# Gather and scatter interleaved tile by tile on TensorE, and all target one-hots loaded instead of three of eight made by VectorE

## What is computed

```python
# block 0: five layers over the edges
h = leaky(x @ W1[l] + b1[l]) @ W2[l] + b2[l]
e = leaky(edge_attr @ We1[l] + be1[l]) @ We2[l] + be2[l]
msg = h[src] * e * dot_scale[l]
agg = segment_sum(msg, dst, num_segments=n)
x = layernorm(x + agg * res_w[l]) * ln_g[l] + ln_b[l]
...
# block 3: one more pass over the edges
msgs = relu(node_inputs[src] + edge_inputs)
agg = segment_sum(msgs, dst, num_segments=n)
```

## Time and profile before

| what | value |
|---|---|
| median of 3 runs | 7844.31 us (7841.6 to 7846.52) |
| the profiled execution | 7817.12 us, its span 7815.2 us |
| PE matmul busy | 6285.5 us (80%) |
| PE weight load busy | 5013.5 us (64%) |
| VectorE busy | 5308.1 us (68%) |
| ScalarE busy | 2933.7 us (38%) |
| GpSimd busy | 2771.1 us (35%) |
| HBM | read 815.28 MB, written 278.78 MB |

### The profile page before, as it was taken

One profiled execution on the slowest core, in us unless ns is written; L12 is line 12 of the kernel. 1 busy time (PEld: TensorE's weight loads), 2 busy tenths in 40 slices (PEclk: granted clock), 3 DMA queues, 4 the chain that ended last, 5 costly groups with the idle time before them and its releaser, 6 DMA issues. The chain is left out here.

```text
span 7815.2 us, 276543 instructions
## 1 busy us (share of the span) xinstructions
PE 6285.5 (80%) x87510; PEld 5013.5 (64%) x87511; DVE 5308.1 (68%) x15345; ACT 2933.7 (38%) x5054; POOL 2771.1 (35%) x4280
## 2 busy tenths in 40 slices
PE   4888888846666588788788788788789998999887
PEld 3666666634444377677677677677776776777676
DVE  7555554579999777677677677677865554555677
ACT  2444444424444433333333333233653332333333
POOL 2666666643333144344344344344000000000343
PEclk9888888865555699899899899799768998999999
DMA  2666666622222577577577577577441111111576
GB/s 78 172 180 181 182 179 177 182 72 73 71 73 71 187 191 191 140 193 196 138 196 193 139 193 196 133 194 192 158 178 51 68 60 44 68 60 60 138 202 174
DMA packets 1403296, 1098.82 MB, mean 141 GB/s; under 512 B 1012406, under 2 KB 1171821, under 8 KB 1393467
## 3 DMA queue, kind: packets, MB, share of 16 engines
q1 hardware_dynamic: 887994, 797.65, 33.3%
q0 software_dynamic: 224768, 240.90, 12.7%
q10 hardware_dynamic: 290304, 57.05, 4.0%
HBM read 815.28 MB, written 278.78 MB: 140 GB/s over the span
## 5 line engine op out<-in xcount | busy, mean ns | idle before, releaser
L544 POOL DMA_DIRECT2D big<-rows x2592 | 1415.2, 546 | 3721.9 <-issue 2284.6
L1309 PE MATMUL ps<-big 128*128 128x64 bf16 x20736 | 1292.7, 198 | 377.7 <-issue 356.3
L1296 PE MATMUL ps<-big 128*128 128x64 bf16 x41472 | 1418.2, 196 | 100.2 <-DVE big L1783 57.5
L1296 PEld LDWEIGHTS ps<-big 128*128 128x128 fp8e4 x41472 | 1338.4, 100 | 175.4 <-issue 135.5
L1309 PEld LDWEIGHTS ps<-big 128*128 128x128 bf16 x20736 | 985.7, 99 | 643.9 <-issue 431.1
L814 POOL DMA_INDIRECT rows<-big x800 | 1022.9, 1279 | 606.3 <-issue 360.9
L1018 ACT CAST big<-big 128x512 bf16<-128x512 f32 x720 | 445.1, 618 | 1293.4 <-DVE big L1796 1230.4
L1796 DVE TENSOR_TENSOR big<-ps,big 128x512 f32<-128x512 f32 x720 | 497.8, 691 | 608.3 <-PE ps L1296 594.1
L1255 PE MATMUL ps<-identb,big 128*128 128x128 bf16 x2304 | 472.6, 308 | 359.9 <-DVE big L1684 353.6
L1573 DVE SCALAR_TENSOR_TENSOR big<-big 128x1000 f32<-128x1000 f32 (+1 forms) x300 | 359.5, 1198 | 579.1 <-ACT big L905 435.5
L1212 PEld LDWEIGHTS ps<-big 128*125 128x125 f32 (+1 forms) x4800 | 682.6, 212 | 101.5 <-issue 57.6
(11 more groups left out here) (263 smaller groups left out, 9350.4 us busy)
## 6 DMA issues: line engine op xcount, KB each, us to landing
big<-ohsD SPq DMA_DIRECT2D x432, 512.0 KB, 3.7
big<-ohdD SPq DMA_DIRECT2D x432, 320.0 KB, 4.1
big<-rows POOLq DMA_DIRECT2D x2592, 32.0 KB, 3.6
big<-rows SPq DMA_DIRECT2D x2592, 32.0 KB, 3.5
big<-maskD SPq DMA_DIRECT2D x50, 1600.0 KB, 6.7
big<-rows ACTq DMA_DIRECT2D x1728, 32.0 KB, 3.3
big<-keyT SPq DMA_DIRECT2D x100, 488.3 KB
maskD<-big SPq DMA_DIRECT2D x25, 1600.0 KB, 6.2
```

Source lines behind the costliest of these rows:

```text
L544: eng.dma_start(edge[:, s.r, j, :], rows[bass.ds(v[s.r * (hi - lo) + j - lo], P), col]).then_inc(landed[s.r], 16)
L1296: last = pe.matmul(pG[g.r][:, j * D:(j + 1) * D], ohsR[:, g.r, at:at + P].bitcast(F8), slices[:, g.r, q // QUAD, (3 * k + c) * D:(3 * k + ...
L1309: last = pe.matmul(pacc[:, bass.ds(w[j], D)], hot[:, g.r, j * P:(j + 1) * P], parts[:, g.r, c, j * D:(j + 1) * D], start=False, stop=False ...
```

## The change

The target one-hots of all eight tiles are stored in `ohdD` and loaded in each pass; `remake`, its semaphore `hot_made`, and POOL's `dstl` go. An `ohdD` load of two groups grows from 320 to 512 KB, and so does its share of the stores in the unpacking stage. On TensorE, `turn_over` takes the place of `scatter` and `gather`: both sets of waits stand at the start of a step, and then for each tile j come the six gather matmuls of group s - 1 and the three scatter matmuls of group s - 5. `gathered` is signalled by the last gather matmul, which is three matmuls before the step's end. The lags, buffers and all other engines' loops are as before.

```diff
@@ -74,8 +74,6 @@
 CW = NP // CUTS
 NQ = TILES // QUAD
 RAW = 3
-KEEP = 5
-MADE = GT - KEEP
 TURNS = -(-W // 4)
 CTS = 4
 ROWSUMS = 11
@@ -113,7 +111,7 @@
         keyT = dram("keyT", (ET, EP))
         blkT = dram("blkT", (ET, EP), BF16)
         ohsD = dram("ohsD", (NG, P, 2 * GT * P), U8)
-        ohdD = dram("ohdD", (NG, P, KEEP * P), BF16)
+        ohdD = dram("ohdD", (NG, P, GT * P), BF16)
         maskD = dram("maskD", (W, P, NP))
         cntD = dram("cntD", (W, P, NP), U16)
...
@@ -405,7 +398,6 @@
         res_ready = sem("res_ready")
         mid_ready = sem("mid_ready")
         lo_ready = sem("lo_ready")
-        hot_made = sem("hot_made")
         hot_loaded = [sem(f"hot_loaded{r}") for r in range(RING // 2)]
         craw_loaded = [sem(f"craw_loaded{r}") for r in range(RAW)]
         over_made = sem("over_made")
@@ -660,7 +652,7 @@
                 sp.wait_ge(hots_ready, i * 2 + 2)
                 hold(sp)
                 sp.dma_start(ohdD[bass.ds(i, 1)].rearrange("o p f -> (o p) f"),
-                             ohD[:, r % 2, 0:KEEP, :].rearrange("p a b -> p (a b)")).then_inc(dst_stored[r % 2], 16)
+                             ohD[:, r % 2, :, :].rearrange("p a b -> p (a b)")).then_inc(dst_stored[r % 2], 16)
 
...
@@ -697,7 +689,7 @@
                 if not s.known or s.i >= RING:
                     sp.wait_ge(scattered, base + s.lag(RING).i + 2)
                     hold(sp)
-                sp.dma_start(hot[:, s.r:s.r + 2, 0:KEEP * P], ohdD[bass.ds(s.i, 2)].rearrange("g p f -> p g f")).then_inc(hot_loaded[s.r // 2], 16)
+                sp.dma_start(hot[:, s.r:s.r + 2, :], ohdD[bass.ds(s.i, 2)].rearrange("g p f -> p g f")).then_inc(hot_loaded[s.r // 2], 16)
 
             def load_pass(base, col):
...
@@ -828,7 +820,6 @@
                     pool.wait_ge(hots_ready, i * 2 - 2)
                     hold(pool)
                 span = bass.ds(i * GT, GT)
-                pool.tensor_tensor(dstl[:, span], rowst[:, r, :, 1], valid[:, span], ALU.mult)
                 for k in range(2):
                     last = pool.tensor_tensor(idm[:, r % 2, k * GT:(k + 1) * GT], rowst[:, r, :, k], valid[:, span], ALU.mult)
                 last.then_inc(ids_masked, 1)
@@ -1280,35 +1271,49 @@
                 for b in range(4):
                     pe.matmul(bank(b), zerob[:, :], zerob[:, 0:1].to_broadcast([P, 512]), start=True, stop=False, skip_group_check=True)
 
-            def gather(s, base, nth):
+            def gather_ready(g, base, nth):
+                pe.wait_ge(ohs_loaded[g.r // 2], (nth * TRIPS + g.t) * 16 + 16)
+                pe.wait_ge(sliced, base + g.i + 1)
+                if not g.known or g.i >= RING:
+                    pe.wait_ge(m_ready, base + g.lag(RING).i + 1)
+                hold(pe)
+
+            def gather(g, j):
+                q = j // QUAD
+                for k in range(2):
+                    at = ((q * 2 + k) * QUAD + j % QUAD) * P
+                    for c in range(3):
+                        last = pe.matmul(pG[g.r][:, j * D:(j + 1) * D], ohsR[:, g.r, at:at + P].bitcast(F8),
+                                         slices[:, g.r, q, (3 * k + c) * D:(3 * k + c + 1) * D],
+                                         start=(k + c == 0), stop=(k + c == 3))
+                return last
+
+            def scatter_ready(g, base, nth):
+                pe.wait_ge(lo_ready, base + g.i + 1)
+                pe.wait_ge(hot_loaded[g.r // 2], (nth * TRIPS + g.t) * 16 + 16)
+
+            def scatter(g, j, w):
+                for c in range(3):
+                    last = pe.matmul(pacc[:, bass.ds(w[j], D)], hot[:, g.r, j * P:(j + 1) * P], parts[:, g.r, c, j * D:(j + 1) * D],
+                                     start=False, stop=False, skip_group_check=True)
+                return last
+
+            def turn_over(s, w, base, nth):
+
+                to, of = s.lag(S_LAG), s.lag(G_LAG)
+                if s.live(S_LAG):
+                    scatter_ready(to, base, nth)
                 if s.live(G_LAG):
-                    g = s.lag(G_LAG)
-                    pe.wait_ge(ohs_loaded[g.r // 2], (nth * TRIPS + g.t) * 16 + 16)
-                    pe.wait_ge(sliced, base + g.i + 1)
-                    if not g.known or g.i >= RING:
-                        pe.wait_ge(m_ready, base + g.lag(RING).i + 1)
-                    hold(pe)
-                    for q in range(0, GT, QUAD):
-                        for j in range(q, q + QUAD):
-                            for k in range(2):
-                                at = ((q // QUAD * 2 + k) * QUAD + j - q) * P
-                                for c in range(3):
-                                    last = pe.matmul(pG[g.r][:, j * D:(j + 1) * D], ohsR[:, g.r, at:at + P].bitcast(F8),
-                                                     slices[:, g.r, q // QUAD, (3 * k + c) * D:(3 * k + c + 1) * D],
-                                                     start=(k + c == 0), stop=(k + c == 3))
-                    last.then_inc(gathered, 1)
-
-            def scatter(s, w, base, nth):
+                    gather_ready(of, base, nth)
+                for j in range(GT):
+                    if s.live(G_LAG):
+                        got = gather(of, j)
+                    if s.live(S_LAG):
+                        put = scatter(to, j, w)
+                if s.live(G_LAG):
+                    got.then_inc(gathered, 1)
                 if s.live(S_LAG):
-                    g = s.lag(S_LAG)
-                    pe.wait_ge(lo_ready, base + g.i + 1)
-                    pe.wait_ge(hot_made, base + g.i + 1)
-                    pe.wait_ge(hot_loaded[g.r // 2], (nth * TRIPS + g.t) * 16 + 16)
-                    for j in range(GT):
-                        for c in range(3):
-                            last = pe.matmul(pacc[:, bass.ds(w[j], D)], hot[:, g.r, j * P:(j + 1) * P], parts[:, g.r, c, j * D:(j + 1) * D],
-                                             start=False, stop=False, skip_group_check=True)
-                    last.then_inc(scattered, 1)
+                    put.then_inc(scattered, 1)
 
             with pe.Fori(0, LAYERS) as l:
                 pe.wait_ge(x_ready, l + 1)
@@ -1341,8 +1346,7 @@
                 def body(s):
                     if s.r % 2 == 0:
                         two[:] = blocks(PE, s.i)
-                    scatter(s, two[s.r % 2], l * NG, l)
-                    gather(s, l * NG, l)
+                    turn_over(s, two[s.r % 2], l * NG, l)
 
                 steps(pe, body)
                 pe.drain().then_inc(summed, 1)
...
@@ -1759,15 +1762,6 @@
                 dve.tensor_tensor(tabp[2], tres, tabp[1], ALU.subtract).then_inc(tab_lo, 1)
                 dve.wait_ge(tab_lo, nth + 1)
 
-            def remake(s, base):
-                if s.live(2):
-                    g = s.lag(2)
-                    if not g.known or g.i >= RING:
-                        dve.wait_ge(scattered, base + g.lag(RING).i + 1)
-                        hold(dve)
-                    dve.tensor_tensor(hot[:, g.r, KEEP * P:].rearrange("p (a b) -> p a b", a=MADE), each(iota1b[:, 0:P], MADE),
-                                      over(dstl[:, bass.ds(g.i * GT + KEEP, MADE)], P), ALU.is_equal).then_inc(hot_made, 1)
@@ -1843,7 +1837,6 @@
                     message(s, l * NG, "edge", l)
                     rest(s, l * NG, "edge")
                     lower(s, l * NG)
-                    remake(s, l * NG)
 
                 steps(dve, body)
                 lc = Chain(dve, l_chain, l * END)
```

More of the change, by code:

```diff
@@ L255, in graph_kernel @@
         ohsT = carve(2, 2 * GT * P, dt=U8)
-        dstl = big[:, BIG - TILES // 2:].bitcast(BF16)
         dq = carve(NQ, 2)
@@ L261, in graph_kernel @@
         total = carve(W)
-        assert carve.at[0] <= BIG - TILES // 2
         rowjunk = ps[:, 0:NP]
@@ L1356, in body @@
                         two[:] = blocks(PE, s.i)
-                    scatter(s, two[s.r % 2], base, nth)
-                    gather(s, base, nth)
+                    turn_over(s, two[s.r % 2], base, nth)
                 steps(pe, body)
@@ L1867, in body @@
                     lower(s, base)
-                    remake(s, base)
                 steps(dve, body)
```

## The result

The changed kernel takes 7546.07 us (median of 4 runs, 7504.43 to 7555.36) against 7845.42 us for the kernel before (4 runs, 7841.6 to 7849.61): a ratio of 0.9608, 95% interval 0.9571 to 0.9645. The forecast was 7475 us in a range of 7380 to 7680, so the sign and the range held, and 71 of the 370 us didn't come.

The account below looks back on a forecast made before the run. PE's own instruction stream was taken as the bound; with four limits near 12, layers at 12.4 us a turn (305 less) and the last pass at 11.7 (65 less) give 370 us less: 7475 us, range 7380 to 7680.

Parts of the forecast that it names:

- PE's instruction stream as the bound: Edge passes: scatter's register instructions starve the array, about 180 ns a tile for 88 ns of matmuls; interleaving hides them.
- Rival (b): Scatter's register instructions aren't hidden by the interleaving, PE keeps 14.1 us a turn: 7844 us, within 15; chance 0.07.
- PE's floor of 12.0 a turn: Layers: interleaving lowers PE's floor from 14.1 to about 12.0 us a turn, bounds 11.4 and 14.1; last pass near 11.6.
- VectorE's relief: Edge passes: one-hots no longer made give nothing alone; VectorE's floor falls from about 2.7 to 2.2 us a group.
- SyncE's 12.05 us a turn: Layers: SyncE's own issuing work doesn't shrink, so no turn can be shorter than 12.05 us; last pass 10.7.
- The late load: Edge passes: larger ohdD loads land 4.8 to 5.3 us after issue instead of 4.1; turn of 11.9 to 12.7 us.
- rival (a): DMA engines or late ohdD loads hold the loop at about 13.2 us a turn: 7664 us; chance 0.18.
- Rival (c): Slower: ohdD landing lengthens the loop from 7.0 us on; with 8 us, 8060 us in all; chance 0.06.
- DMA traffic: Edge passes: engine work grows from 41.2 to 45.9 engine-us a group, a floor of 11.5 us a turn.
- Unpacking: Unpacking stage: POOL loses a small operation and ohdD stores grow; zero, at most 5 us either way.
- The sum: Layers 305 us less and last pass 65 less, together 370 less: 7475 us; chance 0.69.
- 12.4 a turn: Layers: four limits near 12 (12.0, 12.05, 11.5, 11.9 to 12.7) don't overlap perfectly, so 12.4 us a turn was taken.

Follow-up runs that it names:

- Fixed addresses: Kernel before, old order, but scatter tile j adds into block j, without PE's register instructions and table reads (target block choice left out): 7348.99 us, 0.9396.
- four loaded: Kernel before with the interleaved TensorE order, four target one-hots of eight loaded and four made by VectorE: 7388.22 us, 0.9438 against the kernel before.
- five: Kernel before with the interleaved TensorE order alone, five target one-hots loaded and three made by VectorE as before: 7420.49 us, 0.9491.
- edges ahead: Changed kernel with ScalarE's two edge loads issued one group earlier, some from wrong rows: 7494.33 us, 0.9597 against the kernel before.

## Why the prediction was right, and where it was off

**PE's instruction stream as the bound: right.** Fixed addresses bring the scatter's loads from 1.36 to 0.76 us, and the interleaving brings the tile's pitch to the 263 ns worked out. Rival (b) is gone with the timeline. PE's floor of 12.0 a turn was too high: four loaded, the last pass runs at 413.9/143.5 x 4 = 11.5. (The prediction's own terms, 14.1 less 1.9, give 12.2 and not 12.0; and it charged the table reads for a lead of 0.25 us at a step's end, where the step shown above had half a us.) In the layers its term set nothing, since other limits stood above it; in the last pass its 11.6 set the sum.

**VectorE's relief: right that it gives nothing alone** (1.0041), wrong in the next clause, that its lower floor "is what lets PE's new pace through". With all of its comparisons kept VectorE is busy 348.6 of 400 us, and the loop is faster.

**SyncE's 12.05 us a turn: consistent, not proved.** Three kernels with different VectorE and DMA work, all with SyncE next to never waiting, come to 11.95 us a turn (fixed addresses, layer 2: 428.7/143.5 x 4), 12.1 (four loaded) and 12.2 (five); less its waits, SyncE's own work is 11.9 to 12.1. One turn of SyncE with fixed addresses, from the first of these loads to the third, is 11.93 us, filled by its issues, their register instructions and the read of the addresses:

```profile
3402.87 0.38 SPq L693 DMA_DIRECT2D big<-ohsD  x1
...
3409.54 0.39 SPq L693 DMA_DIRECT2D big<-ohsD  x1
...
3414.80 0.38 SPq L693 DMA_DIRECT2D big<-ohsD  x1
```

No layer of any kernel was shorter than 427.7 us. But each attempt to relieve SyncE loaded ScalarE or POOL, and the loop then waited for that queue, so what a layer would take with a free SyncE stays open. In the changed kernel itself SyncE waits 19.3 us in 31.6 turns, 0.6 a turn; there something above it decides.

**The late load: the right kind, the wrong one.** I expected `ohdD` to land at 4.8 to 5.3 us, and it did at 5.1; PE waits for it 23.6 us in 400. But I set only that load's landing against its room. The edge loads on ScalarE have two steps of lead, the steps became shorter, their landing went from 3.3 to 4.0 us (5.7 at most), and nearly half of the messages came late. With one step more of lead these waits went, and up to 13 of the last pass's missing 20 us came back (440.6 to 427.7, where 421 was forecast) and up to 4 us a layer of the 8 that were missing there (452.8 to 448.7, for 445); "up to", because the pieces of ScalarE's loads were cheaper in that run as well. It is rival (a) in kind, "late loads" through another load than the one it names, and in the layers at about a quarter of its size: 12.6 where the forecast was 12.4 and the rival 13.2. Rival (c) didn't come: the median landing of `ohdD` was 5.0 to 5.1 us in every pass and 7.0 its point, though the longest single one, in layer 1, took 6.9.

**DMA traffic: right in the layers, a little small in the last pass, and not a constant.** Forecast were 45.9 engine-us a group and a floor of 11.5 us a turn. Measured over the whole of layer 2: 0.91 x 16 x 454.2/143.5 = 46.1; layer 1 gives 46.8. Over the whole last pass it was 0.97 x 16 x 440.6/143.5 = 47.7, a floor of 11.9, and with edges ahead, for the same bytes, 0.98 x 16 x 427.7/143.5 = 46.7.

```profile
7082.80:7523.30 440.50, 333.58 (x10266) 319.96 (x10267) 311.16 (x711) 177.85 (x285) 224.56 (x420) 0.99 0.97 251
```

The queues of 3290 to 3690 (packets, MB, share of 16 engines) say where it went:

```profile
q1 hardware_dynamic: 88199, 78.03, 65.4%
...
q10 hardware_dynamic: 36057, 8.22, 12.6%
```

ScalarE's 256-byte pieces take 12.6% of 16 x 400 us for 8.22 MB, 25.1 ns each, where they took 20.7. So a busy time taken from a stretch at a share of 0.73 was too small a price for this one at 0.93. That fuller engines make a piece dearer is the likely reason and not the whole of it: in the last pass the same share of 0.99 went with 26.8 ns and with 22.8. The forecast of 11.7 a turn in the last pass is what the interleaving alone reaches (418.5 us). The loads had raised only the DMA term, to 11.5, which stayed under PE's 11.6 and so added nothing to that sum; measured, they took the rest, 12.3 for 11.7.

**Unpacking: 6 us, said to be at most 5.** 860.9 became 867.0 us, and every kernel that stores eight has 866 us or more. Of the kernels that store four or five, seven took 859.2 to 861.5 and one, five with one edge load moved to POOL, took 866.6; so the larger store is the likely cause and not the only one.

**The sum.** Layers 268 for 305, last pass 45 for 65, unpacking 6 for 0; the sorting took 35 us more in the profiled execution and the dense blocks 8, both inside the spread of the other runs. The 12.4 a turn was the highest single limit, SyncE's 12.05, with a margin inside the range of the landing that nothing priced. That 12.6 came so near is partly luck: ScalarE's late edge loads, for one, stood in no term.

**What stays open.** How much of the gain with edges ahead is the lead's and how much the cheaper pieces'; and how the remaining 13 us a layer of what the loads cost (448.7 against 436.1 us) divide between `ohdD`'s landing in front of the step, the hand-over from VectorE (PE waited 52.2 us for L1777 before the gather) and the DMA engines' pace. Doing edges ahead and four loaded together was not tried.

## What to carry to other kernels

Where an engine's sequencer works out addresses for short matmuls, put independent array work between them: that alone gave 5.1% here, and a timeline of the weight loads' pitch shows it. Don't trade an idle engine's work for traffic once the loop is about to run faster: the same loads that cost 14 us in the six passes of the slow loop cost 105 us in those of the fast one. Before speeding a loop up, list for every load its lead over its first reader at the new pace and its landing at the new DMA share, and for every issuing queue its us a turn; here the shortest lead was the one that broke. And don't take the longest wait for the largest loss: removing 115 us of waiting a layer gave 4 us.

## What the runs showed that I had not expected

- One edge load moved from SyncE to ScalarE cost 164 us (7546 to 7710), although ScalarE is busy 155 of 400 us: an issue stands in its instruction stream (0.90 us for two) ahead of the copies, and busy shares don't count it.
- The DMA engines' work for a 256-byte piece on ScalarE's queue rose from 20.7 to 25.1 ns between a share of 0.73 and one of 0.93 (22.8 to 26.8 at 0.99), and the traffic ended at 256 to 263 GB/s with a share of 0.99. The Trainium skill (DMA: Bandwidth & Descriptors, Specifications) gives about 358 GB/s for a core; these runs, with their mix of 256-byte and larger pieces, stopped well below it.
- The sorting stage, with the same instructions, ended between 1717 and 1760 us.
